# A fifth gated product moved to ScalarE and GpSimd, two small products on part of TensorE's rows, and a new order

## The chip, the core and the metric

The kernel runs on one core of a Trainium2 chip. The metric is the device time of one execution in microseconds (us). The core has five engines, each with its own in-order queue: TensorE (PE in the profile) multiplies matrices out of SBUF into PSUM; VectorE (DVE), ScalarE (ACT) and GpSimd (POOL) work elementwise; SyncE (SP) here only issues DMAs. They are ordered among each other by semaphores alone. Of PSUM's eight banks of 128x512 f32, four ("work0" to "work3") rotate among all the products, two are g_bank and two are du_bank.

## The reference

For x of 16 sequences ("batches") of 1024 positions and 256 channels:

```
def ffn(x):  h = silu(x @ wg.T) * (x @ wu.T); return h @ wd.T      # 256 -> 768 -> 256, integer weights / 127
def mamba(x):
    z, params = x @ W_z.T, x @ W_params.T                          # params: 64 for dt, 16 unused, 16 for C
    dt = softplus(params[..., :64] @ W_dt.T + b_dt)
    u  = silu(causal_conv4(x, conv_w))
    # for each of 16 states n and 256 channels e, along the 1024 positions:
    #   h[t+1] = exp(dt A) h[t] + (exp(dt A) - 1) / A * u[t]
    y  = sum_n C[n] * h[n];  return ((y + u * D) * silu(z)) @ W_out.T
x = x + 0.5 * ffn(layernorm(x)); x = x + mamba(layernorm(x)); x = x + 0.5 * ffn(layernorm(x))
```

## The kernel before, in words

Channels (of which there are two halves h of 128) lie on the partitions for the recurrence, and positions run along the free axis, in two chunks c of 512 for the matrix products. All 16 batches are unrolled, and several are in flight: while batch b's recurrence runs, the first feed-forward network of batch b+1 and the second of batch b-2 or so fill the other engines.

The recurrence of a batch is 32 units (16 states by two halves). A unit is: `ex` on ACT (decay = exp(dt A), line 1042), a DMA `bc` that spreads a row of C over the partitions (SP), `scan` on DVE (tensor_tensor_scan over 1024 positions, line 1281), `cm` on DVE (the scan's result times 1/A times C, into one of TERMS = 2 buffers, line 1317), and `cm` on POOL (adding it to acc, line 1121). The scan runs on differences of u, and the part of y that this leaves out is made by one product per half and chunk, `rm` (line 847): params' C rows (partitions 64 to 79) times a small matrix 1/A. `ai` and `aj` (DVE, lines 1253 and 1259) take it from PSUM into acc. The first and the last batch run their scans in halves of 512.

A feed-forward network has for each chunk six products `ga` and six `up` (PE, line 781; four f16 matmuls each, 128x128 by 128x512), then for each of the six parts m: `si` on ACT (silu of ga, line 924), and up times silu in one of two ways. For m in OWN, `sh` on DVE multiplies out of PSUM in one instruction (line 1234). For m in POOLED, `sc` on ACT copies up out of PSUM (line 932), and `hp` on POOL multiplies it by the silu in SBUF (line 1089). `dn` (PE, line 793) then multiplies all six parts of a chunk by wd. The up product's PSUM bank is free after `sh` or `sc`.

dt is made by `dt` on PE (line 840): a matmul of wdt_t by params over all 128 partitions. Rows 0 to 63 hold W_dt, row 96 of wdt_t holds b_dt with a row of ones in params, and the rest are zeros. `rm` likewise uses wrm_t over all 128 partitions, zero outside rows 64 to 79. `da` (ACT, lines 1000 to 1005), `dl` (ACT, lines 1012 to 1017) and `dp` (POOL, lines 1076 to 1081) make the softplus; they need another activation table than silu does, and ACT loads a table (line 860) wherever its order goes from one set to the other.

The order is written out by hand: tables (ROW for every batch; HEAD, SECOND, LATE and TAIL for batches 0, 1, 14 and 15) give each event a place, in units of a recurrence unit; `schedule()` sorts all events by it, and each engine takes the events that are its own in that one order. The four banks go to products in that order too (`Counts`, the bank that comes free first by place).

```
POOLED = {1: (0, 1, 2, 4), 2: (0, 1, 2, 4)}
OWN = {f: tuple(m for m in range(HM) if m not in POOLED[f]) for f in POOLED}
```

Of the kernel before, what the change touches and what calls it, by code (L numbers as in the profile page):

```python
# [65 lines left out]
C_ROW, ONE_ROW = 64, 96  # L66
# [72 lines left out]
    "gate": [19.958, 32.034],  # L139
    "scan": [0.213, 1.117, 2.593, 4.358, 5.349, 7.197, 7.625, 8.34, 9.445, 10.358, 11.389, 11.995, 13.207, 13.906,  # L140
        15.384, 15.903, 16.687, 18.32, 19.159, 19.899, 20.145, 20.943, 21.856, 22.753, 23.339, 24.496, 25.654, 26.37,
        27.576, 28.502, 29.719, 31.321],
    "cm": [0.763, 2.558, 3.307, 4.92, 5.936, 7.602, 7.645, 9.259, 9.973, 11.247, 11.68, 12.76, 13.675, 14.855, 15.701,
        16.238, 17.889, 19.05, 19.701, 20.074, 20.454, 21.836, 22.241, 23.055, 23.983, 24.827, 25.814, 27.11, 27.713,
        28.928, 30.427, 31.538],
    "bc": [-1.292, -0.471, 1.458, 1.927, 2.074, 2.339, 2.605, 3.54, 3.597, 5.394, 5.595, 6.81, 7.858, 7.893, 12.423,
        12.62, 13.422, 14.507, 15.09, 15.693, 17.865, 19.808, 20.366, 20.415, 20.994, 21.672, 21.766, 22.738, 24.616,
        26.245, 26.666, 29.544],
    "ex": [-0.864, 0.407, 0.698, 2.552, 2.752, 3.176, 4.127, 7.005, 7.156, 8.287, 8.437, 9.472, 12.612, 12.613,
        13.633, 13.837, 14.032, 14.734, 14.892, 15.535, 20.244, 20.502, 21.59, 21.848, 22.003, 22.603, 23.104, 23.195,  # L150
        23.408, 24.045, 26.871, 29.393],
    "op": [36.6, 36.073, 36.94, 40.339],
    "rc": [35.127, 34.564, 36.399, 40.194],
    "ra": [34.909, 35.474, 39.379, 41.765],
# [15 lines left out]
    "T2": [-15.367, 4.54],  # L170
    "Te2": [-20.05, 2.156],
    "ga1": [-82.598, -69.485, -56.827, -53.465, -52.215, -34.173, -35.219, -29.252, -28.985, -22.303, -21.242,
        -16.595],
    "si1": [-58.331, -72.212, -58.391, -50.493, -49.241, -46.574, -37.798, -27.857, -31.608, -23.71, -19.783, -19.2],
    "up1": [-84.097, -72.985, -62.385, -50.056, -47.935, -32.398, -31.353, -27.452, -24.043, -21.497, -14.128,
        -11.262],
    "sc1": [-86.862, -66.411, -70.046, -47.336, -37.827, -26.261, -25.69, -18.657],
# [12 lines left out]
    "dt": [-10.318, 10.19, -2.737, 15.485],  # L190
    "da": [-16.899, 6.405, -12.887, 11.631],
    "dl": [-14.958, 9.24, -11.602, 12.717],
    "dp": [-10.273, 9.633, -9.525, 12.01],
    "rm": [0.73, 16.404, -0.749, 18.186],
    "ai": [0.111, 12.635, -10.309, 16.146],
    "aj": [0.623, 13.391, -7.852, 18.484],
    "u0": [-11.158],
    "dt0": [-8.994],
    "d": [-8.345, 11.96],
    "db": [-6.135, 13.086],  # L200
    "gate": [14.708, 31.922],
    "scan": [-3.781, 0.11, 1.556, 2.829, 3.481, 4.451, 5.102, 5.805, 6.741, 7.694, 8.338, 8.954, 9.864, 10.183,
        12.705, 13.767, 14.812, 16.319, 18.496, 19.822, 20.516, 20.961, 22.117, 22.793, 23.175, 24.454, 24.679,
        25.637, 28.915, 29.55, 31.209, 31.699],
# [1150 lines left out]
```

## Time and profile before

| | |
|---|---|
| median of 3 runs | 2249.23 us (2248.78 to 2249.27) |
| profiled execution's own time | 2249.76 us |
| its span, first to last instruction | 2248.0 us |
| granted TensorE clock, mean | 0.979 |
| instructions | 27771 |

Busy time is the union of an engine's instruction spans. Matmuls overlap in a pipeline, so a PE that looks busy may still have short gaps in its stream; these are read from the distance between the starts of two matmuls. The whole falls into a head up to the first scan at 80.9 us, batch 0's recurrence up to 218.9 us, fourteen batches alike, the last batch from 2067.7 us, and a tail after the last scan starts at 2197.3 us.

### The profile page before, as it was taken

Reading aid. Unit: us, or ns where it says so; the run is one execution under the profiler, and the core shown is the slowest. Engines: PE = TensorE matmul, PEld = TensorE weight load, DVE = VectorE, ACT = ScalarE, POOL = GpSimd, SP = SyncE. Lnnn points to the kernel's source line nnn. Section 1 sums busy time; section 2 is a strip of 40 time slices with the busy share of each in tenths; the row PEclk is TensorE's granted clock in tenths of the full one; section 3 lists DMA queues with packets and bytes.
Section 4 is the critical chain, followed back from the end, with each engine's and each line's share of the span. In section 5 each row is a group of like instructions: output and inputs, shape, how many; then the busy total and the mean of one; then the engine's idle time right before and its main releaser. Section 6 shows DMA issues by size and latency. Waiting matters only on the chain.

```text
span 2248.0 us, 27771 instructions
## 1 busy us (share of the span) xinstructions
PE 2122.2 (94%) x8708; PEld 1282.5 (57%) x8708; DVE 2125.0 (95%) x2297; ACT 1957.5 (87%) x2900; POOL 1885.0 (84%) x1446
## 2 busy tenths in 40 slices
PE   7977999999999999999999999999999999998488
PEld 4543656656565665656566565656656565565245
DVE  2699999999999999999999999999999999999992
ACT  5989898999989899898989989899898989996782
POOL 2688889898988989898898988889899888988663
PEclk9988999999999999999999999999999999999689
DMA  2122343444344344434444443444444444433120
GB/s 93 58 66 84 133 151 132 158 143 150 123 159 145 129 160 141 151 132 150 141 142 151 141 150 133 149 142 141 151 145 140 149 142 142 146 133 121 61 75 29
DMA packets 112024, 291.15 MB, mean 130 GB/s; under 512 B 11201, under 2 KB 45314, under 8 KB 111874
## 3 DMA queue, kind: packets, MB, share of 16 engines
q1 hardware_dynamic: 111874, 289.35, 37.8%
q8 instruction: 69, 1.13, 0.2%
q14 instruction: 81, 0.66, 0.1%
HBM read 271.49 MB, written 17.83 MB: 129 GB/s over the span
## 4 chain that ended last, share of the span: by engine, by line
PE 34%; DVE 17%; ACT 15%; issue 13%; POOL 10%; DVEq 0%; POOLq 0%; ACTq 0%
PE work L793 14%; PE work L781 11%; DVE g_bank L1281 9%; POOL acc L1121 7%; DVE ring L1317 5%; ACT ring L1042 4%; ACT L860 3%; PE work L810 3%; ACT xt_lo L911 2%; PE work L803 2%; PE work L761 1%; POOL hid L1089 1%; PE work L847 1%; ACT hid L932 1%; ACT odd L924 1%
## 5 line engine op out<-in xcount | busy, mean ns | idle before, releaser
L1281 DVE TENSOR_TENSOR_SCAN g_bank<-du_bank,ring 128x1024 f32<-128x1024 f32 (+1 forms) x512 | 1099.0, 2152 | 6.4 <-ACT ring L1042 1.4
L1121 POOL TENSOR_TENSOR acc<-acc,ring 128x1024 f32<-128x1024 f32 x512 | 1023.8, 2000 | 70.1 <-DVE ring L1317 44.4
L793 PE MATMUL work<-wd_t,hid 128*128 128x256 f32 x3072 | 679.8, 379 | 3.5 <-DVE hid L1234 2.9
L1317 DVE SCALAR_TENSOR_TENSOR ring<-g_bank,inv_a,ring 128x1024 f32<-128x1024 f32 (+1 forms) x576 | 660.5, 1152 | 10.1 <-POOL acc L1121 7.6
L793 PEld LDWEIGHTS work<-wd_t,hid 128*128 128x128 f32 x3072 | 583.7, 190 | 108.2 <-issue 20.7
L1042 ACT ACTIVATE ring<-dt,a_coef 128x1024 f32<-128x1024 f32 (+1 forms) x576 | 582.7, 1047 | 8.2 <-DVE g_bank L1281 7.1
L1089 POOL TENSOR_TENSOR hid<-hid,odd 128x512 f32<-128x512 f32 x256 | 277.8, 1094 | 131.6 <-ACT hid L932 94.0
L781 PE MATMUL work<-xt_hi,wg_t 128*128 128x512 f16 x768 | 296.3, 386 | 15.6 <-ACT hid L932 6.7
L781 PE MATMUL work<-xt_hi,wu_t 128*128 128x512 f16 x768 | 294.5, 383 | 15.6 <-ACT odd L924 8.4
L860 ACT ACT_TABLE_LOAD x231 | 296.4, 1283 | 4.1
L781 PE MATMUL work<-xt_lo,wg_t 128*128 128x512 f16 x768 | 295.3, 385 | 0.0
L781 PE MATMUL work<-xt_lo,wu_t 128*128 128x512 f16 x768 | 294.2, 383 | 0.0
L924 ACT ACTIVATE odd<-work 128x512 f32<-128x512 f32 x384 | 220.3, 597 | 60.3 <-PE work L781 58.6
L832 PE MATMUL work<-xt,tap_diag 128*128 128x512 f32 x512 | 227.6, 592 | 0.0
L932 ACT ACTIVATE hid<-work 128x512 f32<-128x512 f32 x256 | 148.9, 588 | 18.8 <-PE work L781 10.4
L781 PEld LDWEIGHTS work<-xt_hi,wg_t 128*128 128x128 f16 x768 | 75.6, 98 | 152.0 <-ACT hid L932 23.9
L832 PEld LDWEIGHTS work<-xt,tap_diag 128*128 128x128 f32 x512 | 96.8, 189 | 112.6 <-issue 106.5
L781 PEld LDWEIGHTS work<-xt_hi,wu_t 128*128 128x128 f16 x768 | 75.6, 98 | 117.4 <-issue 20.1
L781 PEld LDWEIGHTS work<-xt_lo,wu_t 128*128 128x128 f16 x768 | 75.7, 99 | 111.0 <-issue 39.2
L803 PE MATMUL work<-wo_t,acc 128*128 128x256 f32 x512 | 124.4, 388 | 6.8 <-POOL acc L1112 6.0
L781 PEld LDWEIGHTS work<-xt_lo,wg_t 128*128 128x128 f16 x768 | 76.1, 99 | 83.4 <-issue 19.8
L810 PE MATMUL work<-xt,wz_t 128*128 128x512 f32 x256 | 122.1, 598 | 0.3 <-DVE hid L1234 0.2
(98 smaller groups left out, 2610.8 us busy)
## 6 DMA issues: line engine op xcount, KB each, us to landing
ring<-c_rows SPq DMA_DIRECT2D x448, 512.0 KB, 3.7
ring<-c_rows SPq DMA_DIRECT2D x64, 256.0 KB, 3.1
x_in<-L_attn_x SPq DMA_DIRECT2D x30, 512.0 KB, 3.9
out<-x_fin SPq DMA_DIRECT2D x30, 512.0 KB, 4.2
x_fin<-L_attn_x SPq DMA_DIRECT2D x2, 512.0 KB, 5.9
c_rows<-params SPq DMA_DIRECT2D x32, 32.0 KB, 3.3
out<-x_in SPq DMA_DIRECT2D x2, 512.0 KB, 3.0
ring<-L_ffn_w_gate SPq DMA_DIRECT2D x1, 768.0 KB, 5.8
```

The source lines that it names most:

```text
L781: last = pe.matmul(dst[:], w[:, k, m * P:(m + 1) * P], part_[:, k, :], start=(k == 0 and i == 0), stop=(k == EH - 1 and i == 1))
L793: last = pe.matmul(dst[:, j * E:(j + 1) * E], hid[:, K.unit[f, bt, c, m] % HIDS, t:t + P], wd_t[:, m, :], start=(m == 0), stop=(m == HM - 1))
L810: last = pe.matmul(dst[:], wz_t[:, k, h * P:(h + 1) * P], xt[:, k, KW - 1 + c * CH:KW - 1 + (c + 1) * CH], start=(k == 0), stop=(k == EH - 1))
L832: last = pe.matmul(dst[:], tap_diag[:, h, k, :], xt[:, h, k + c * CH:k + (c + 1) * CH], start=(k == 0), stop=(k == KW - 1))
L860: nc.scalar.preload_act_table_set(name)
L924: nc.scalar.activation(sil[:, K.at["silu", ev][1] % SILUS, :], bank(job)[:], ACT.Silu, scale=GATE_SCALE).then_inc(freed(job), 1)
L932: nc.scalar.activation(hid[:, K.unit[ev[1:]] % HIDS, :], bank(job)[:], ACT.Copy, scale=H_SCALE).then_inc(freed(job), 1)
L1042: nc.scalar.activation(dst, dt[bt % 2][:, h, t], ACT.Exp, scale=a_coef[:, h, s:s + 1]).then_inc(S["decay"], 1)
L1089: nc.gpsimd.tensor_tensor(v, v, sil[:, k, :], ALU.mult).then_inc(S["product"], 1)
L1121: nc.gpsimd.tensor_tensor(v, v, shaped(bt, cg[:, K.number[ev[1:]] % TERMS, :]), ALU.add).then_inc(S["summed"], 1)
L1281: scan = nc.vector.tensor_tensor_scan(g, du_h, d_h, first[0], ALU.add, ALU.mult)
L1317: nc.vector.scalar_tensor_tensor(v, g, inv_a[:, h, s:s + 1], c_row, ALU.mult, ALU.mult).then_inc(S["weighted"], 1)
```

## The change

One of six parts more, m = 3, is in POOLED in both networks: for it `sh` on DVE gives way to `sc` on ACT and `hp` on POOL. `dt` multiplies partitions 0 to 63 alone, `rm` partitions 64 to 79 alone, both out of one tile wk_t; b_dt is added as the bias operand of the two activations that read dt's bank; the fills of zeros and ones for wdt_t, wrm_t and params go, and so does the DMA of b_dt into row 96, for which two small DMAs put it on the partitions. All five tables have new numbers.

```diff
-POOLED = {1: (0, 1, 2, 4), 2: (0, 1, 2, 4)}
+POOLED = {1: (0, 1, 2, 3, 4), 2: (0, 1, 2, 3, 4)}
...
-    "sh1": [-27.982, -24.382, -20.207, -19.555],
+    "sh1": [-27.097, -21.572],
...
-        wdt_t, wrm_t = sb("wdt_t", [P, E]), sb("wrm_t", [P, E])
+        wk_t = sb("wk_t", [P, E])
...
-            sp.wait_ge(s_pads, 1)
-            sp.dma_start(wdt_t[ONE_ROW:ONE_ROW + 1, :], b_dt.rearrange("(o e) -> o e", o=1)).then_inc(w_landed, 16)
...
+                    sp.dma_start(dt_bias[:, h:h + 1], b_dt.rearrange("(h p o) -> h p o", p=P, o=1)[h]).then_inc(w_landed, 16)
...
-                    pe.matmul(dst[:], wdt_t[:, h * P:(h + 1) * P], params[:, c * CH:(c + 1) * CH],
+                    pe.matmul(dst[:], wk_t[0:R, h * P:(h + 1) * P], params[0:R, c * CH:(c + 1) * CH],
...
-                    pe.matmul(dst[:], wrm_t[:, h * P:(h + 1) * P], params[:, c * CH:(c + 1) * CH],
+                    pe.matmul(dst[:], wk_t[C_ROW:PROWS, h * P:(h + 1) * P], params[C_ROW:PROWS, c * CH:(c + 1) * CH],
...
-                    nc.scalar.activation(y, bank(job)[:], ACT.Abs).then_inc(S["sp_exp"], 1)
+                    nc.scalar.activation(y, bank(job)[:], ACT.Abs, bias=dt_bias[:, h:h + 1]).then_inc(S["sp_exp"], 1)
...
-                    nc.scalar.activation(sp_r[:, c, :], bank(job)[:], ACT.Relu).then_inc(freed(job), 1)
+                    nc.scalar.activation(sp_r[:, c, :], bank(job)[:], ACT.Relu,
+                                         bias=dt_bias[:, h:h + 1]).then_inc(freed(job), 1)
...
-            for t in (wdt_t[R:P, :], wrm_t[:], xt[:, :, 0:KW - 1], u[0][:, :, 0:1], u[1][:, :, 0:1]):
+            for t in (xt[:, :, 0:KW - 1], u[0][:, :, 0:1], u[1][:, :, 0:1]):
...
-            then(nc.vector.memset(params[R:P, :], 0.0))
-            nc.vector.memset(params[ONE_ROW:ONE_ROW + 1, :], 1.0).then_inc(s_pads, 1)
+            nc.vector.memset(ones[:], 1.0).then_inc(s_pads, 1)
```

What the new tables do to the order of an ordinary batch, by sorting both sets (between the first scans of batches 6 and 7):

| per batch | before | after |
|---|---|---|
| `cm` directly behind its `scan` on DVE (of 32) | 4 | 7 |
| `scan` directly behind the last `cm` on DVE (of 32) | 10 | 11 |
| `sh` on DVE | 8 | 4 |
| `sc` on ACT, `hp` on POOL, each | 16 | 20 |
| changes of activation table on ACT | 14 | 12 |
| `dt` and `rm` next to each other on PE | 2 | 2 |
| places where PE goes into or out of a `dt` or `rm`, or from one to the other | 14 | 14 |

In batches 0 and 15 the changes of table go from 16 and 17 to 15 and 17.

## Rows read from the trace of the kernel before

**Rows 1.** The page's busy time of each engine over the whole span.
```profile
PE 2122.2 (94%) x8708; PEld 1282.5 (57%) x8708; DVE 2125.0 (95%) x2297; ACT 1957.5 (87%) x2900; POOL 1885.0 (84%) x1446
```

**Rows 2.** Busy time in stretches: batch 0, a middle batch, the last batch, the tail.
```profile
core 0: us, PE busy (x) PEld busy (x) DVE busy (x) ACT busy (x) POOL busy (x), PEclk, DMA share, GB/s
80.90:218.90 138.00, 109.93 (x366) 57.17 (x364) 134.27 (x199) 121.40 (x194) 107.57 (x81) 0.88 0.23 72
...
1000.00:1132.20 132.20, 130.52 (x546) 79.46 (x545) 131.36 (x133) 120.35 (x177) 117.71 (x91) 1.00 0.42 144
2067.70:2197.30 129.60, 83.43 (x306) 49.33 (x306) 123.48 (x174) 91.32 (x137) 88.14 (x59) 0.78 0.22 69
2197.30:2248.00 50.70, 42.54 (x194) 28.64 (x194) 10.95 (x22) 15.37 (x27) 15.91 (x15) 0.99 0.09 32
```

**Rows 3.** Two lines: count, ns min/median/max, first and last start.
```profile
L980 ACT ACTIVATE dt<-dt x16: 206/218/218, 75.3 to 2059.5; 128x2 f32<-128x2 f32 x16
...
L847 PE MATMUL work<-params,wrm_t x128: 592/592/1222, 77.7 to 2060.2; 128*128 128x512 f32 x128
```

**Rows 4.** Groups of instructions: count, busy us, mean ns, idle time before them.
```profile
L1234 DVE SCALAR_TENSOR_TENSOR hid<-odd,work 128x512 f32<-128x512 f32 x128 | 86.6, 676 | 35.4 <-PE work L781 27.1 <-ACT odd L924 8.3
L932 ACT ACTIVATE hid<-work 128x512 f32<-128x512 f32 x256 | 148.9, 588 | 18.8 <-PE work L781 10.4 <-PE work L793 8.3
L1089 POOL TENSOR_TENSOR hid<-hid,odd 128x512 f32<-128x512 f32 x256 | 277.8, 1094 | 131.6 <-ACT hid L932 94.0 <-ACT odd L924 37.6
L860 ACT ACT_TABLE_LOAD x231 | 296.4, 1283 | 4.1
```

**Rows 5.** VectorE in order of time in a middle batch: start us, length us, instruction.
```profile
903.18 0.68 DVE L1234 SCALAR_TENSOR_TENSOR hid<-odd,work 128x512 f32<-128x512 f32 x1
903.77 2.29 DVE L1281 TENSOR_TENSOR_SCAN g_bank<-du_bank,ring 128x1024 f32<-128x1024 f32 x1
906.10 1.28 DVE L1317 SCALAR_TENSOR_TENSOR ring<-g_bank,inv_a,ring 128x1024 f32<-128x1024 f32 x1
907.42 2.30 DVE L1281 TENSOR_TENSOR_SCAN g_bank<-du_bank,ring 128x1024 f32<-128x1024 f32 x1
909.62 0.40 DVE L1192 BATCH_NORM_STATS2 stats<-x_fin 128x6 f32<-128x256 f32 x1
...
913.77 1.27 DVE L1317 SCALAR_TENSOR_TENSOR ring<-g_bank,inv_a,ring 128x1024 f32<-128x1024 f32 x1
914.95 0.42 DVE L1192 BATCH_NORM_STATS2 stats<-x_mid 128x6 f32<-128x256 f32 x1
```

**Rows 6.** TensorE in order of time in a middle batch: start, length, instruction, count.
```profile
905.13 10.52 PE L793 MATMUL work<-wd_t,hid 128*128 128x256 f32 x48
915.49 1.04 PE L761 MATMUL work<-ident,normed 128*128 128x128 f32 x8
916.37 0.38 PE L781 MATMUL work<-xt_hi,wg_t 128*128 128x512 f16 x1
...
957.08 0.38 PE L781 MATMUL work<-xt_lo,wu_t 128*128 128x512 f16 x1
957.29 1.88 PE L823 MATMUL work<-xt,wp_t 128*80 128x512 f32 x4
959.01 3.60 PE L832 MATMUL work<-xt,tap_diag 128*128 128x512 f32 x8
...
973.66 7.03 PE L832 MATMUL work<-xt,tap_diag 128*128 128x512 f32 x16
980.53 0.38 PE L781 MATMUL work<-xt_hi,wu_t 128*128 128x512 f16 x1
```

**Rows 7.** Who waited for whom in the middle batch: us, times, longest.
```profile
POOL hid L1089 <- ACT hid L932: 4.2, 3, 2.6
...
POOL acc L1121 <- DVE ring L1317: 1.3, 2, 0.7
```

More of the change, by code:

```diff
@@ L65 @@
 OUT_SCALE = 1.0 / Q
-C_ROW, ONE_ROW = 64, 96
+C_ROW = 64
 PROWS = C_ROW + N
 ROW = {
[60 rows of a table removed]
[L139 to L154, printed above, removed]
[60 rows of a table added]
+    "gate": [18.967, 32.939],
+    "scan": [1.713, 2.257, 2.986, 4.146, 4.572, 5.864, 7.012, 7.944, 9.04, 9.371, 9.903, 10.488, 11.413, 12.548,
+        13.986, 14.924, 15.326, 16.515, 17.338, 20.028, 21.592, 22.338, 23.077, 24.46, 26.143, 26.895, 28.276, 29.192,
+        29.513, 30.542, 31.1, 32.213],
+    "cm": [1.732, 2.653, 3.608, 4.305, 5.35, 6.496, 7.48, 8.646, 9.251, 9.496, 10.037, 10.555, 11.872, 13.299, 14.429,
+        14.956, 16.331, 17.075, 19.594, 20.924, 22.058, 23.075, 24.297, 25.159, 26.486, 27.703, 28.432, 29.244,
+        30.033, 30.795, 31.451, 32.477],
+    "bc": [-4.2, -4.16, -4.006, -3.21, 0.386, 0.915, 1.732, 2.182, 2.392, 3.187, 3.301, 3.753, 4.304, 5.867, 6.113,
+        6.19, 7.682, 8.527, 9.387, 10.17, 11.075, 11.154, 11.157, 15.289, 15.297, 15.546, 15.886, 17.945, 19.042,
+        19.336, 19.853, 23.54],
+    "ex": [0.178, 0.564, 1.216, 1.894, 1.916, 2.557, 4.626, 5.295, 5.57, 6.13, 6.151, 6.363, 11.173, 11.707, 12.11,
+        12.438, 12.466, 12.481, 13.956, 14.355, 20.173, 21.199, 21.509, 21.737, 22.117, 24.504, 26.081, 26.294,
+        28.025, 29.706, 30.926, 31.546],
+    "op": [35.434, 37.665, 38.094, 40.995],
+    "rc": [34.012, 34.754, 35.23, 39.134],
+    "ra": [34.239, 35.401, 38.637, 42.266],
@@ L170 @@
[L170 to L177, printed above, removed]
@@ L190 @@
[L190 to L204, printed above, removed]
@@ L211 @@
-    "ex": [-8.608, -6.948, -6.05, -5.862, -5.855, 4.815, 4.873, 6.05, 6.076, 7.394, 7.638, 7.925, 7.967, 8.908,
-        11.188, 12.662, 13.589, 13.668, 14.752, 14.895, 15.559, 17.738, 19.621, 20.167, 20.251, 20.554, 21.038,
-        24.989, 25.313, 27.508, 27.709, 30.016],
+    "sj1": [-387.901, -356.697, -344.097, -296.764, -288.913, -264.857, -254.411, -219.314],
+    "ln1": [-275.223, -195.556],
+    "lr1": [-155.576, -144.062],
+    "lx1": [-242.188, -132.422],
+    "T1": [-133.328, -72.186],
@@ new lines @@
+    "Te1": [-164.432, -72.268],
+    "Ts1": [-125.334, -62.84],
+    "Tl1": [-145.91, -62.687],
+    "sj2": [-72.591, -67.207, -48.943, -41.538, -17.684, -14.93, -11.969, -10.384],
+    "ln2": [-41.102, -10.247],
+    "lr2": [-60.509, -12.932],
+    "lx2": [-37.296, -4.509],
+    "T2": [-38.61, 0.718],
+    "Te2": [-37.221, -0.303],
+    "ga1": [-109.896, -104.426, -89.445, -78.956, -73.427, -71.163, -43.782, -42.324, -39.773, -37.955, -27.025,
+        -16.68],
+    "si1": [-110.23, -116.044, -104.464, -74.437, -67.206, -63.217, -61.921, -55.489, -53.129, -36.069, -31.275,
+        -29.214],
@@ new lines @@
+    "up1": [-100.363, -99.877, -85.23, -84.23, -74.024, -61.949, -46.579, -38.732, -38.609, -34.552, -34.243,
+        -13.399],
+    "sc1": [-81.282, -109.585, -99.71, -90.591, -72.871, -60.615, -41.92, -35.684, -32.141, -34.513],
+    "hp1": [-94.81, -136.005, -141.235, -123.565, -70.446, -57.912, -55.432, -54.024, -42.459, -39.977],
+    "sh1": [-81.724, -26.095],
+    "dn1": [-57.404, -56.835, -9.131, -7.992],
+    "rs1": [-62.779, -62.62, -18.344, -16.105],
+    "rp": [-69.661, -65.874, -29.164, -26.921],
@@ new lines @@
+    "pm": [-33.635, 2.485],
+    "pe": [-34.314, 0.93],
+    "cw": [-25.519, -9.579],
+    "cv": [-18.27, 13.668, -15.382, 14.595],
+    "us": [-29.139, 7.38, -26.157, 8.195],
+    "z": [14.392, 14.521, 13.665, 14.729],
+    "zs": [7.516, 8.299, 6.526, 9.413],
+    "dt": [-19.009, 3.89, -12.409, 18.794],
+    "da": [-29.876, 4.451, -25.087, 9.53],
+    "dl": [-29.689, 4.911, -22.362, 10.797],
+    "dp": [-38.898, 1.881, -36.432, 9.856],
+    "rm": [-10.724, 19.613, -12.307, 14.763],
+    "ai": [-22.206, 10.113, -24.612, 5.756],
@@ new lines @@
+    "aj": [-21.514, 11.09, -21.899, 9.505],
+    "u0": [-25.56],
+    "dt0": [-18.61],
+    "d": [-37.361, 5.706],
+    "db": [-18.761, 11.885],
+    "gate": [16.192, 34.043],
+    "scan": [-20.353, -12.568, -10.188, -8.53, -4.075, -3.217, -1.657, -1.25, -0.515, 0.788, 2.068, 3.005, 4.064,
+        5.342, 10.624, 11.441, 14.111, 16.388, 17.639, 19.619, 20.426, 21.029, 21.512, 21.871, 22.431, 23.811, 26.418,
+        27.533, 29.718, 29.853, 31.559, 32.56],
+    "cm": [-17.648, -11.754, -9.72, -8.118, -3.975, -2.93, -1.384, -1.081, 0.3, 1.5, 2.191, 3.075, 4.626, 7.645,
+        10.875, 12.309, 14.52, 16.456, 17.673, 19.624, 20.517, 21.283, 21.526, 22.049, 22.745, 23.921, 27.401, 27.794,
+        29.806, 30.137, 31.647, 33.701],
@@ new lines @@
+    "bc": [-22.003, -20.4, -20.249, -14.875, -13.449, -9.893, -9.856, -8.768, -7.776, -5.161, -4.537, -0.877, 0.64,
+        0.685, 3.84, 4.593, 4.767, 6.956, 9.237, 9.286, 10.145, 10.276, 10.542, 11.831, 13.456, 17.393, 18.653,
+        19.334, 20.433, 22.717, 26.552, 27.458],
+    "ex": [-18.534, -17.323, -16.727, -6.736, -0.326, 0.275, 0.459, 1.334, 2.804, 4.433, 5.215, 5.538, 5.541, 7.778,
+        7.966, 10.997, 11.267, 12.593, 12.836, 13.343, 13.717, 14.317, 14.925, 15.941, 16.229, 16.866, 18.018, 20.076,
+        21.473, 21.527, 28.816, 31.247],
@@ L249 @@
-    "zs": [-1.007, 4.337, 5.547, 11.264],
-    "dt": [-6.237, -6.058, -1.385, -4.164],
-    "da": [-11.111, -10.953, -3.604, -6.002],
-    "dl": [-5.549, -9.873, -2.707, -4.263],
-    "dp": [-5.386, -9.003, -2.63, -4.436],
-    "rm": [-2.629, -1.527, -3.197, -0.48],
-    "ai": [-5.778, -5.883, -6.449, -3.278],
-    "aj": [-2.577, -5.595, 1.0, -2.635],
-    "u0": [-6.096],
-    "dt0": [-1.571],
+    "sj1": [-101.526, -89.664, -84.422, -83.375, -70.436, -70.115, -68.598, -67.105],
+    "ln1": [-72.468, -63.986],
@@ new lines @@
+    "lr1": [-87.228, -70.016],
+    "lx1": [-67.762, -48.865],
+    "T1": [-60.689, -39.201],
+    "Te1": [-66.181, -43.768],
+    "Ts1": [-52.284, -36.733],
+    "Tl1": [-64.094, -38.931],
+    "sj2": [-29.098, -28.232, -23.773, -23.4, -18.3, -16.614, -15.401, -14.934],
+    "ln2": [-19.073, -14.814],
+    "lr2": [-20.241, -15.955],
+    "lx2": [-18.774, -16.607],
+    "T2": [-11.59, -10.019],
+    "Te2": [-17.22, -16.425],
+    "ga1": [-42.345, -41.537, -35.661, -34.644, -34.217, -33.835, -34.833, -32.361, -30.89, -28.82, -22.326, -13.985],
@@ new lines @@
+    "si1": [-51.124, -52.582, -38.526, -34.213, -36.056, -33.14, -36.978, -32.671, -28.986, -28.416, -24.252,
+        -23.136],
+    "up1": [-44.016, -41.856, -40.643, -39.411, -38.689, -31.938, -35.189, -31.266, -23.953, -22.406, -17.596,
+        -13.468],
+    "sc1": [-56.411, -52.398, -44.875, -43.887, -42.772, -37.686, -31.004, -30.244, -26.816, -24.813],
+    "hp1": [-64.735, -47.989, -44.484, -38.234, -38.452, -44.317, -32.056, -30.838, -28.943, -28.918],
+    "sh1": [-37.737, -21.608],
@@ new lines @@
+    "dn1": [-23.069, -20.97, -11.982, -11.883],
+    "rs1": [-27.933, -25.556, -20.885, -18.466],
+    "rp": [-34.767, -26.823, -22.017, -18.494],
+    "pm": [-11.409, -9.105],
+    "pe": [-16.359, -15.877],
+    "cw": [-21.533, -13.545],
+    "cv": [-7.812, -6.318, -7.531, -4.243],
+    "us": [-8.978, -11.079, -8.654, -9.172],
+    "z": [10.324, 5.906, 6.416, 13.613],
+    "zs": [8.71, 2.816, 3.639, 9.639],
+    "dt": [-9.241, -9.007, -3.116, -4.136],
+    "da": [-15.362, -13.753, -4.195, -8.098],
@@ L259 @@
+    "dl": [-14.603, -12.28, -3.84, -7.345],
+    "dp": [-9.462, -10.261, -2.915, -7.755],
+    "rm": [-1.984, -3.883, -8.106, 2.181],
+    "ai": [-1.091, -4.444, -4.502, 2.069],
+    "aj": [-0.192, -3.986, 0.684, 2.645],
+    "u0": [-7.747],
+    "dt0": [-0.37],
 }
 LATE = {
[20 rows of a table removed]
[20 rows of a table added]
 }
 TAIL = {
[19 rows of a table removed]
-    "gate": [15.254, 44.043],
-    "scan": [-0.319, 0.278, 0.623, 1.403, 2.382, 3.653, 5.734, 6.239, 7.481, 9.201, 9.722, 10.891, 11.786, 12.922,
-        14.222, 14.507, 15.214, 15.567, 16.279, 18.584, 20.236, 21.371, 22.376, 24.181, 25.341, 27.461, 29.689,
-        32.064, 34.041, 35.127, 36.83, 39.326],
@@ L314 @@
-    "ex": [0.802, 1.479, 1.687, 2.664, 3.071, 3.088, 3.396, 5.612, 5.697, 5.885, 6.371, 6.883, 7.3, 7.778, 9.361,
-        9.592, 9.67, 11.252, 15.483, 16.846, 17.11, 18.659, 20.09, 20.234, 20.425, 22.32, 22.83, 26.878, 28.561,
-        33.456, 33.752, 34.973],
-    "op": [20.494, 24.225, 53.337, 54.333],
-    "rc": [16.63, 19.283, 45.948, 48.68],
-    "ra": [15.756, 20.623, 56.439, 56.856],
[19 rows of a table added]
+    "gate": [20.075, 65.881],
+    "scan": [1.295, 2.306, 2.847, 4.031, 7.258, 8.112, 9.075, 9.872, 10.504, 10.807, 11.979, 12.281, 12.343, 13.184,
+        15.056, 17.372, 17.792, 20.534, 22.398, 23.231, 28.471, 32.713, 36.093, 39.195, 40.704, 42.028, 42.676,
+        47.145, 48.341, 54.999, 58.796, 60.92],
@@ new lines @@
+    "cm": [1.549, 2.449, 3.876, 6.405, 7.884, 8.778, 9.372, 10.022, 10.668, 11.373, 11.998, 12.296, 12.44, 14.083,
+        16.441, 17.761, 19.93, 20.891, 22.399, 27.524, 30.903, 33.057, 36.865, 40.12, 40.755, 42.463, 44.84, 48.133,
+        48.663, 58.548, 60.266, 65.147],
+    "bc": [-8.291, -4.714, -2.747, 8.503, 11.188, 11.549, 11.761, 12.111, 13.936, 14.947, 15.55, 17.751, 19.282,
+        20.406, 21.225, 22.813, 24.784, 26.389, 27.908, 33.999, 38.276, 39.089, 39.966, 60.034, 60.726, 62.727,
+        69.926, 79.698, 81.515, 84.993, 86.916, 110.724],
@@ L320 @@
+    "ex": [-0.086, 1.246, 1.909, 2.27, 2.541, 3.889, 5.22, 5.84, 7.245, 7.267, 8.781, 9.599, 11.542, 11.761, 11.956,
+        16.416, 16.754, 19.719, 21.931, 23.81, 26.937, 27.175, 31.24, 32.251, 32.88, 33.005, 40.278, 48.337, 51.826,
+        51.827, 63.136, 63.776],
+    "op": [27.484, 29.349, 78.22, 80.408],
+    "rc": [27.191, 29.695, 84.667, 89.314],
+    "ra": [25.823, 26.577, 91.894, 104.369],
 }
@@ L564, in macaron_kernel @@
         part_ident = sb("part_ident", [P, P], F16)
-        consts = sb("consts", [P, 2 * TJ + 1 + EH + 1])
+        FLAG = 2 * TJ + 1 + 2 * EH
+        consts = sb("consts", [P, FLAG + 2])
         minus_half, eps = consts[:, 0:TJ], consts[:, TJ:2 * TJ]
         ones, d_skip = consts[:, 2 * TJ:2 * TJ + 1], consts[:, 2 * TJ + 1:2 * TJ + 1 + EH]
+        dt_bias = consts[:, 2 * TJ + 1 + EH:2 * TJ + 1 + 2 * EH]
         a_coef = sb("a_coef", [P, EH, N])
@@ L572, in macaron_kernel @@
         carry = sb("carry", [P, 2, N, EH, 1])
-        flag = consts[0:1, 2 * TJ + 1 + EH:].bitcast(I32)
-        flag_f = stats[0:1, 0, 0, 0:1]
+        flag = consts[0:1, FLAG:FLAG + 1].bitcast(I32)
+        flag_f = consts[0:1, FLAG + 1:FLAG + 2]
         inv_a_u = hid[:, 0, 0:EH * PROWS].rearrange("p (h n) -> p h n", h=EH)
@@ L655, in freed @@
             return free[K.bank[job]]
-        LANDED = 16 * 9
+        LANDED = 16 * 10
         block = ctx.enter_context(nc.Block())
@@ L677, in _ @@
                 (wp_t[:, :, C_ROW:C_ROW + N], W_params[:, R + N:R + 2 * N].rearrange("(k p) m -> p k m", p=P)),
-                (wdt_t[0:R, :], W_dt),
+                (wk_t[0:R, :], W_dt),
                 (wz_t[:], W_z.rearrange("(k p) e -> p k e", p=P)),
@@ L1151, in _ @@
             nc.vector.memset(meanvar[:, :, :, 2:3], -1.0)
-            then(nc.vector.memset(params[R:P, :], 0.0))
-            nc.vector.memset(params[ONE_ROW:ONE_ROW + 1, :], 1.0).then_inc(s_pads, 1)
+            nc.vector.memset(ones[:], 1.0).then_inc(s_pads, 1)
             then(nc.vector.memset(inv_a_u, 0.0))
-            then(nc.vector.memset(ones[:], 1.0))
             dve.wait_ge(s_exp, 1)
```

70 lines of the change are left out of this document (1 added, 69 removed), and 196 rows, old and new, of tables (LATE, ROW, TAIL).

## The prediction

> **What bounds the kernel now.** I read four views in this order. First the page's busy time [rows 1]: DVE 95% and PE 94% of the span, ACT 87%, POOL 84%. Two engines look full, so averages don't tell which sets the pace. Second, an instruction that comes once a batch, the first row of [rows 3]: its sixteen starts lie (2059.5 - 75.3) / 15 = 132.3 us apart. Third, the stretches [rows 2]: in a middle batch of 132.20 us DVE is busy 131.36 us and idle 0.84. In batch 0 and in the last one DVE is the busiest too (134.27 of 138.00, 123.48 of 129.60), with PE far behind. Only the tail belongs to PE (42.54 of 50.70).
>
> Fourth, PE's stream, because its lengths overlap and flatter it. In [rows 6] 48 matmuls of 128x256 f32 start 915.49 - 905.13 = 10.36 us apart in all, 0.216 each; an f16 one of 512 columns takes 0.21; sixteen passes of 128x512 f32 take 980.53 - 973.66 = 6.87, 0.429 each; eight of 128x128 take 916.37 - 915.49 = 0.88, 0.110 each. By the loops (an f32 product is two passes) a batch has 192 for ga and up, 192 for dn, 32 for op and 8 for the low parts at 0.216 (91.6 us), 72 at 0.429 for cv, z, pm, dt and rm (30.9 us), and 48 at 0.110 (5.3 us): 127.8 us of 132.2. So PE has 4.4 us a batch in hand, DVE less than one. DVE sets the period; PE is close behind.
>
> **The change, part by part.**
>
> *The fifth pooled product, on DVE.* An `sh` takes 903.77 - 903.18 = 0.59 us of DVE from start to start [rows 5] (its 676 ns in [rows 4] overlap the next instruction). Four go per batch, 64 in all. Those that count lie between the first and the last scan: two each from the first networks of batches 1 to 15 and from the second ones of batches 0 to 14, thus 60. 60 x 0.59 = 35.4 us, 2.36 a batch.
>
> *The order, on DVE.* `cm` needs its scan's result. Right behind the scan it starts 906.10 - 903.77 = 2.33 us after it; with another instruction between, that one starts 909.62 - 907.42 = 2.20 after the scan [rows 5]. So a bare neighbour costs 0.13. A scan right behind a `cm` costs 907.42 - 906.10 = 1.32 against 914.95 - 913.77 = 1.18 with something between, 0.14. The removed `sh` were also such fillers: sorted, the new tables have three more bare pairs of the first kind and one more of the second, 3 x 0.13 + 0.14 = 0.53 us a batch, 7.4 in fourteen and, at half that in the two batches of half scans, some 8 in all. The net of DVE is 35.4 - 8 = 27.4 us, 1.83 a batch; the floor of the period falls from 132.2 to 130.4.
>
> *ACT.* Four `sc` more at 588 ns are 2.35 us; two table loads fewer at 1283 ns are 2.57 [rows 4]. ACT goes from 120.35 busy us a batch [rows 2] to 120.1 of 130.4, 92%. Nothing, and DVE is its cover. In batch 0 it is one load less, in the last none.
>
> *POOL.* Four `hp` more at 1094 ns [rows 4] are 4.38 us: from 117.71 [rows 2] to 122.1 of 130.4, 94%. Its idle time falls from 14.5 to 8.3 us a batch. Behind an `hp` that waits for its `sc` is the `cm` addition, and behind that DVE's `cm` two units later, as there are two buffers. In the middle batch POOL waited 4.2 us for ACT's copies and 1.3 for DVE [rows 7], well within 8.3. I take 0.2 us a batch, 3 in all, for this closer coupling; the bounds are nothing and the slow rival below.
>
> *dt and rm on part of the rows.* The trace has no product on fewer than 128 partitions. The nearest row is the one with fewer columns: pm (128*80) starts 957.29 - 957.08 = 0.21 us behind a full product and leaves to one after 959.01 - 957.29 = 1.72 for four passes, 0.43 each, no more than a full one [rows 6]. So I take nothing. The bounds: at best the two neighbouring dt-rm pairs of a batch run side by side, each product being 2 x 0.429, and save 2 x 0.86 = 1.7 us of PE; at worst each of the 14 places where the kind of product changes makes PE finish before it goes on. An rm pass is 592 ns long in the median [rows 3], while starts are 429 apart [rows 6], thus 0.163 us a place, 2.3 a batch. Either is PE's alone, whose 127.8 stand under 130.4.
>
> The Trainium skill speaks against this change here: "TensorEngine Tiling (Array Packing)", section Tiling Modes, says that going over to another tiling mode, not just another tile, empties TensorE first. By it the worst bound is the case, and PE needs 127.8 + 2.3 = 130.1 of the 130.4. No run here shows it yet.
>
> *Bias, fills, DMAs.* The bias rides on two activations that are there anyway. The two fills and the DMA that go, and the two small DMAs that come, are in the first 15 us, before the weights are used; ACT and PE work on batch 0's first network there. Nothing; at most 1 us either way.
>
> *Head and tail.* Before the first scan DVE isn't the bound, so the two `sh` of batch 0's first network that go bring nothing. In the tail PE is [rows 2], and the last part, m = 5, stays with DVE, so that the last product needs no trip through ACT and POOL. Nothing, give or take 2 us.
>
> *Sum*, against the profiled execution's own time of 2249.76 (span 2248.0 and 1.8 around it): 2249.8 - 35.4 + 8 + 3 = 2225.4. That execution is 0.5 above the median of its runs, so 2225.
>
> **Rivals.**
>
> *PE becomes the bound, no change.* If row-limited products cost 2.3 us a batch and PE keeps half of its present 4.4 us of gaps, which come from waiting for ACT to free banks, the period is 127.8 + 2.3 + 2.2 = 132.3: 2250, give or take 6. For it: PE is already 127.8 of 132.2, and a period nearer to its work leaves it less room for waits. Against: most gaps of a slack engine close when it becomes the bound, and pm shows no cost.
>
> *POOL becomes the bound, slower.* The place is POOL's queue in the feed-forward stretch: `hp` waits for `sc`, and the accumulating `cm` of the recurrence stands behind it, so DVE's `cm` waits for "summed". POOL's busy time would be 122.1; as long as its idle time stays under 8.3 us a batch, DVE leads; over 10.1 the kernel is slower than before. Now it is 14.5. If it only falls to 12, the period is 134.1: 14 x 1.9 = 27 us more, about 2276. For it: in the whole run POOL waits 94.0 us for `sc` results [rows 4], and every fourth more asks for more of them. Against: in the middle batch these are only 4.2 us [rows 7]; the rest is in head, tail and batch 0, where they cost nothing.
>
> *More than forecast.* The neighbours run side by side, PE needs 126.1, and the order hides its bare pairs behind waits that go: the full 2.36 us a batch and something of the 0.84 idle, 2249.8 - 35.4 - 4 = 2210, give or take 5. The Trainium skill has the mechanism in "TensorE: Matmul & The Clock Gate", Part 3: products in different row groups overlap, while a lone one of few rows is no shorter. For it: dt has rows 0 to 63, rm 64 to 79, in different banks. Against: PE's gain helps DVE only where DVE waits, which is 0.84 us.
>
> *Row limits do nothing at all*, the same instructions by time: that is within the forecast, as I cost them at nothing.
>
> **Chances.** Forecast (2217 to 2236) 0.55; more 0.13; PE the bound 0.18; POOL the bound 0.14. A measurement tells 0.2%, 4.5 us, from no change. Faster by more than that: 0.55 + 0.13 + 0.4 of PE's 0.18 = 0.75; within: 0.10, nearly all from PE's case; slower: the POOL case and a little of PE's, 0.15. The range is 2206 to 2257: it leaves out 0.03 below and about 0.13 above.
>
> **What would show it.** DVE: 4 `sh` a batch, scans 130.4 to 130.8 us a batch apart, DVE's idle time under 1.2 us in it. ACT: 203 table loads (14 batches with two fewer). POOL: 320 `hp`, 122 us a batch. PE: passes of dt and rm still 0.429 apart, and the next product right behind. The forecast fails if a middle batch's DVE idle time rises over 2.5 us: look then at whether "POOL acc" or "PE work" ended its waits (or ACT's decay, starved by ACT's own waits for PE). If dt and rm stand off their neighbours by 0.1 us or more, the emptying is real. If the batch's period is as said but the time isn't, head or tail moved.

## The result and the profile after

The changed kernel takes 2265.3 us (2263.4 to 2265.5, 4 runs) against 2249.2 before: a ratio of 1.007 with a 95% interval of 1.0053 to 1.0087. It is slower by 16 us, where 24 us less was forecast. The profiled execution's span is 2263.7 us (before 2248.0).

First the page's busy time, to be read beside [rows 1], then the groups that answer to [rows 4], with their counts.

```profile
PE 2150.3 (95%) x8708; PEld 1274.8 (56%) x8708; DVE 2089.9 (92%) x2229; ACT 1965.2 (87%) x2936; POOL 1946.9 (86%) x1510
...
L1234 DVE SCALAR_TENSOR_TENSOR hid<-odd,work 128x512 f32<-128x512 f32 x64 | 43.7, 682 | 70.5 <-PE work L782 70.0 <-issue 0.5
L861 ACT ACT_TABLE_LOAD x203 | 260.4, 1283 | 3.6
```

DVE does 35 us less, as the sum said, and POOL 62 more (64 `hp` of 1.094 us would be 70), and ACT is about where it was (8 more). But PE, which got no product more, is busy 28 us longer, and the 64 `sh` that are left wait 70.0 us for PE's up products where 128 waited 27.1.

Then the stretches, with [rows 2] beside them: batch 0, a middle batch, the last batch, the tail.

```profile
85.60:228.80 143.20, 119.47 (x377) 60.05 (x376) 133.03 (x196) 124.51 (x200) 110.57 (x84) 0.86 0.24 69
...
1028.40:1161.20 132.80, 131.73 (x546) 79.02 (x545) 129.37 (x130) 120.62 (x179) 121.57 (x95) 1.00 0.43 143
...
2088.40:2211.70 123.30, 76.22 (x291) 43.72 (x291) 121.89 (x171) 93.74 (x141) 90.15 (x61) 0.81 0.24 73
2211.70:2263.70 52.00, 44.45 (x204) 31.05 (x202) 9.82 (x20) 13.16 (x24) 18.14 (x17) 1.00 0.09 31
```

The edges are starts of first and last scans, so the span splits. Up to the first scan: 85.6 - 80.9 = +4.7. Batch 0: +5.2. Batches 1 to 14: (2088.4 - 228.8) - (2067.7 - 218.9) = +10.8. Last batch: -6.3. Tail: +1.3. Sum +15.7. In the middle batch DVE is busy 129.37 us, 2.0 less than before, but idle 3.4 instead of 0.84; one `sh` accounts for most of it (VectorE in order of time; the bracket is idle time and what ended it):

```profile
1144.71 0.69 DVE L1234 SCALAR_TENSOR_TENSOR hid<-odd,work 128x512 f32<-128x512 f32 x1 [2.69 <-PE work L782]
```

Why PE is late stands in its own order of time. The first group of rows is PE's matmuls around a `dt` (now L841, 64 rows), the second the weight loads of the same microseconds; [rows 6] has full products.

```profile
1105.40 3.70 PE L833 MATMUL work<-xt,tap_diag 128*128 128x512 f32 x8
1109.03 1.12 PE L841 MATMUL work<-params,wk_t 64*128 64x512 f32 x2
1110.08 2.42 PE L833 MATMUL work<-xt,tap_diag 128*128 128x512 f32 x5
```

```profile
1108.08 0.19 PEld L833 LDWEIGHTS work<-xt,tap_diag 128*128 128x128 f32 x1 [0.24 <-issue]
1109.03 0.29 PEld L841 LDWEIGHTS work<-params,wk_t 64*128 64x128 f32 x2 [0.76 <-issue]
1110.08 0.30 PEld L833 LDWEIGHTS work<-xt,tap_diag 128*128 128x128 f32 x2 [0.76 <-issue]
```

Two passes of `dt` take 1110.08 - 1109.03 = 1.05 us from start to start where two full ones take 0.86, and the load ends an idle time of 0.76 instead of 0.24. The third group is the same place in e2 below, where `dt` has all 128 rows (weight loads; dt is L826 there):

```profile
1087.45 0.19 PEld L818 LDWEIGHTS work<-xt,tap_diag 128*128 128x128 f32 x1 [0.24 <-issue]
1087.88 0.19 PEld L826 LDWEIGHTS work<-params,wdt_t 128*128 128x128 f32 x1 [0.24 <-issue]
1088.31 0.19 PEld L826 LDWEIGHTS work<-params,wdt_t 128*128 128x128 f32 x1 [0.24 <-issue]
1088.74 0.19 PEld L818 LDWEIGHTS work<-xt,tap_diag 128*128 128x128 f32 x1 [0.24 <-issue]
```

There `dt`'s first matmul starts at 1088.31, and its weights went in at 1087.88, while the matmul ahead streamed: a load every 0.43 us, each hidden. In the changed kernel the load of `dt`'s first pass starts only at 1109.03, with the pass itself, and so does that of the first full pass behind it, at 1110.08. The second load of each pair follows 0.11 us later, under the first pass. So two things are paid where the rows in use change: the stream stops (0.09 us), and the first pass has its weight load in the open (0.53 us to the second pass instead of 0.43).

Over thirteen middle batches the distances between starts give 0.09 us more at each of the 14 places where the kind changes, and 0.104 more behind the first pass of each row-limited product (8 a batch). 8 x 0.104 + 14 x 0.09 = 2.1 us a batch. Matched matmul by matmul with e2, the full f32 products that follow a `dt` pay for their first pass too: 0.104 behind the one at 1110.08 and behind one `dn`, 0.055 behind a transpose, 0.26 in all. f16 products pay nothing there. Together that is 2.4 us a batch.

### The profile page after: what moved, and what is told of

Same layout as the page of the kernel before. It is cut to its first block and busy times, and to the rows that moved or that the text cites. A ratio compares the mean times of both kernels' runs of the same rounds, so it can differ in the third digit from the quotient of the medians.

```text
span 2263.7 us, 27746 instructions
## 1 busy us (share of the span) xinstructions
PE 2150.3 (95%) x8708; PEld 1274.8 (56%) x8708; DVE 2089.9 (92%) x2229; ACT 1965.2 (87%) x2936; POOL 1946.9 (86%) x1510
## 5 line engine op out<-in xcount | busy, mean ns | idle before, releaser
L1091 POOL TENSOR_TENSOR hid<-hid,odd 128x512 f32<-128x512 f32 x320 | 346.4, 1093 | 86.4 <-ACT odd L925 56.0
L933 ACT ACTIVATE hid<-work 128x512 f32<-128x512 f32 x320 | 188.7, 592 | 77.2 <-PE work L782 71.5
L833 PE MATMUL work<-xt,tap_diag 128*128 128x512 f32 x512 | 232.5, 602 | 0.7 <-ACT u L970 0.7
L833 PEld LDWEIGHTS work<-xt,tap_diag 128*128 128x128 f32 x512 | 95.0, 190 | 133.3 <-issue 121.3
```

The costliest lines, as they stand in the source:

```text
L833: last = pe.matmul(dst[:], tap_diag[:, h, k, :], xt[:, h, k + c * CH:k + (c + 1) * CH], start=(k == 0), stop=(k == KW - 1))
L933: nc.scalar.activation(hid[:, K.unit[ev[1:]] % HIDS, :], bank(job)[:], ACT.Copy, scale=H_SCALE).then_inc(freed(job), 1)
L1091: nc.gpsimd.tensor_tensor(v, v, sil[:, k, :], ALU.mult).then_inc(S["product"], 1)
```

## The experiments

Times are medians; "before" ran beside each version on its chip, at 2248.9 to 2249.5. e1 to e4, e5 to e8 and e9 to e11 ran on three different chips. The bias on the activations and its DMAs stay as in the changed kernel in all of them.

| | order | pooled parts | dt and rm | us | ratio to before (95%) | us a middle batch |
|---|---|---|---|---|---|---|
| before | old | 4 | 128 rows | 2249.2 | 1 | 132.20 |
| e1 | old | 4 | 64, 16 | 2268.1 | 1.0081 (1.0064 to 1.0097) | 133.33 |
| e3 | old | 5 | 128 | 2292.0 | 1.0187 (1.0170 to 1.0204) | 134.90 |
| e4 | old | 5 | 64, 16 | 2316.2 | 1.0297 (1.0280 to 1.0314) | 137 in eight, 135.3 to 135.6 else |
| after | new | 5 | 64, 16 | 2265.3 | 1.0070 (1.0053 to 1.0087) | 132.77 |
| e2 | new | 5 | 128 | 2228.5 | 0.9906 (0.9890 to 0.9923) | 130.70 |
| e5 | new | 5 | 80, 80 | 2230.1 | 0.9912 (0.9895 to 0.9928) | 130.70 |
| e6 | new | 5 | 64, 128 | 2251.5 | 1.0007 (0.9997 to 1.0016) | 132.21 |
| e7 | new | 5 | 128, 16 | 2244.8 | 0.9982 (0.9972 to 0.9992) | 131.65 |
| e8 | new | 5 | 64, 64 | 2237.5 | 0.9944 (0.9928 to 0.9961) | 131.08 |
| e9 | new | 5 | 64, 64 in pairs alone | 2222.8 | 0.9885 (0.9867 to 0.9903) | 130.20 |

**e1, the row limits alone.** The changed kernel with before's tables and POOLED.

```diff
-POOLED = {1: (0, 1, 2, 3, 4), 2: (0, 1, 2, 3, 4)}
+POOLED = {1: (0, 1, 2, 4), 2: (0, 1, 2, 4)}
```

> The row-limited dt and rm (and the bias) alone, on the old order and four pooled parts. Both theories expect TensorE's passes of dt and rm 0.53 us apart instead of 0.43 and about 0.09 us more at each of the 14 places where TensorE enters or leaves them, 2.1 us a batch. Theory A (these weight loads, no longer hidden, are what made the change slower): TensorE's 4.4 us of gaps a batch are mostly tied to other waits, so half or more of the 2.1 us reaches the period: 2249 + 15 to 30 = 2264 to 2279. Theory B (the new order's own waits are the cause, and TensorE's spare time takes the 2.1 us up): 2248 to 2254.

2268.1, +19: theory A. 1.1 us reach the ordinary period although PE had 4.4 us of gaps; batch 0 takes 3.7 more (141.7 for 138.0).

This run also shows what the extra time belongs to. In its batch 0 two `dt` products, four passes on 64 rows, stand next to each other. PE's matmuls, then the weight loads, in order of time:

```profile
174.38 1.98 PE L825 MATMUL work<-params,wk_t 64*128 64x512 f32 x4
176.29 1.12 PE L817 MATMUL work<-xt,tap_diag 128*128 128x512 f32 x2
```

```profile
174.38 0.29 PEld L825 LDWEIGHTS work<-params,wk_t 64*128 64x128 f32 x2 [0.76 <-issue]
174.92 0.19 PEld L825 LDWEIGHTS work<-params,wk_t 64*128 64x128 f32 x1 [0.24 <-issue]
175.35 0.19 PEld L825 LDWEIGHTS work<-params,wk_t 64*128 64x128 f32 x1 [0.24 <-issue]
176.29 0.30 PEld L817 LDWEIGHTS work<-xt,tap_diag 128*128 128x128 f32 x2 [0.76 <-issue]
```

The passes start at 174.38, 174.92, 175.35 and 175.78, the full product behind them at 176.29: steps of 0.53, 0.43, 0.43 and 0.52. The third and fourth pass have their loads hidden like full ones. So 64 rows as such don't keep a load from starting early; the 0.104 belongs to the first pass behind a stop. The kernel before has it as well, on 128 rows, where `dt` had waited:

```profile
426.68 1.13 PE L840 MATMUL work<-params,wdt_t 128*128 128x512 f32 x2 [0.25 <-ACT xt L898]
427.64 0.38 PE L781 MATMUL work<-xt_hi,wu_t 128*128 128x512 f16 x1
```

427.64 - 426.68 = 0.96 = 0.53 + 0.43. Between 300 and 2000 us all 12 `dt` of the kernel before that start behind such a wait have 0.53 between their passes, the 39 others 0.43.

**e2, full rows in the changed kernel.**

```diff
-        wk_t = sb("wk_t", [P, E])
+        wdt_t, wrm_t = sb("wdt_t", [P, E]), sb("wrm_t", [P, E])
...
-                    pe.matmul(dst[:], wk_t[0:R, h * P:(h + 1) * P], params[0:R, c * CH:(c + 1) * CH],
+                    pe.matmul(dst[:], wdt_t[:, h * P:(h + 1) * P], params[:, c * CH:(c + 1) * CH],
...
-                    pe.matmul(dst[:], wk_t[C_ROW:PROWS, h * P:(h + 1) * P], params[C_ROW:PROWS, c * CH:(c + 1) * CH],
+                    pe.matmul(dst[:], wrm_t[:, h * P:(h + 1) * P], params[:, c * CH:(c + 1) * CH],
```

> The changed kernel with dt and rm over all 128 partitions again (zero-padded weights, as before); fifth pooled part, bias and new order stay. Theory A: the period falls from 132.8 by up to 2.1 us, to 130.7 to 131.5, and batch 0 shortens too: 2235 to 2247. Theory B: TensorE's passes are 0.43 apart again but VectorE's waits stay, period 132.3 to 132.8: 2258 to 2265.

2228.5: 37 us less than the changed kernel and 21 less than before, beyond what theory A had said. The ordinary period falls by 2.07 us (29 us in 14 batches), batch 0 by 4.3, the head by 1.6. The `sh` that waited 2.69 us for PE waits 0.89 here. DVE is idle 1.5 us:

```profile
1008.20:1138.90 130.70, 129.68 (x546) 79.76 (x544) 129.18 (x130) 120.36 (x179) 121.51 (x95) 1.00 0.44 146
```

**e3, the fifth part alone, on the old order.** Its `sc` and `hp` stand where the old trace has the `sh` they replace.

```diff
-    "sh1": [-27.982, -24.382, -20.207, -19.555],
+    "sh1": [-24.382, -19.555],
-    "sc1": [-34.21, -31.112, -28.501, -27.83, -25.852, -25.568, -22.962, -21.819],
+    "sc1": [-34.21, -31.112, -28.501, -28.871, -27.83, -25.852, -25.568, -22.962, -21.083, -21.819],
```

> The fifth pooled part alone: dt and rm over all rows, old order with sc and hp of part 3 put where the old trace has the time of the sh that they replace. If VectorE's 0.59 us for each sh is what counts, as the prediction has it: 2249 - 35 + 8 = 2222 to 2232. Rival C (GpSimd or the longer way through ScalarE holds the bank and the recurrence back): 2250 or more. The two table loads that the new order saves are not saved here, so ScalarE carries 2.4 us more a batch, 93 percent of the period.

2292.0, rival C: the same relief of DVE, placed in this way, makes the old order 43 us slower. DVE is idle 5.1 us of a middle batch, 0.84 before. Half of that is what my slow rival named, `cm` on DVE behind POOL, which was 0.3 us before (waits in us, times, longest):

```profile
DVE ring L1301 <- POOL acc L1107: 2.5, 2, 1.7
DVE x_fin L1226 <- PE work L778: 0.7, 1, 0.7
DVE hid L1218 <- ACT odd L909: 0.4, 1, 0.4
DVE g_bank L1265 <- ACT ring L1028: 0.4, 1, 0.4
```

**e4, both on the old order.** e3's tables in the kernel with row limits.

> Fifth pooled part and row-limited dt and rm, on the old order. Theory A: e3 plus 15 to 30 us. Theory B: e3 plus 0 to 6 us, since the row limits only use up spare time of TensorE; then the rest of the 2265 is the new order's.

2316.2, 24 more than e3, within theory A's range. So the row limits cost 19, 24 and 37 us on the three bases, and the dearest is the one with least room on PE (in a middle batch PE is idle 1.0 us in e2, 1.7 before, 4.0 in e3). About half of e4's 24 is something else: in eight ordinary batches its period is 137 and not 135.3 to 135.6, each with a fall of TensorE's clock (last section).

**e5, 80 rows for both.** The weights are zero where a product has none; the same rows of params.

```diff
-wdt_t[:, h * P:(h + 1) * P]   -wrm_t[:, h * P:(h + 1) * P]
+wdt_t[0:PROWS, ...]           +wrm_t[0:PROWS, ...]            (e5)
+wdt_t[0:R, ...]                                               (e6)
                               +wrm_t[C_ROW:PROWS, ...]        (e7)
+wdt_t[0:R, ...]               +wrm_t[C_ROW:P, ...]            (e8)
```

> e2 (new order, five pooled parts) with dt and rm both on partitions 0 to 79, the weights padded with zeros. Theory D (the weight load of a product on at most 64 partitions, a part of the array, is not begun under the matmul ahead of it, nor the next load under that product; the count of rows as such costs nothing): passes 0.43 us apart, time as e2, 2225 to 2231. Theory E (any count under 128 does it): passes 0.53 apart, 2255 to 2266.

2230.1, and the period is e2's to 0.01 us, as theory D had it and not E: 80 rows cost what 128 do. But this doesn't show D's cause, a load on at most 64 rows that is never begun early. The four passes in e1 speak against it. A price for each change between 128 (or 80), 64 and 16 rows fits all of these runs.

**e6 and e7, dt alone and rm alone.** As the diff above says, the other product on all rows.

> e2 with dt alone on 64 partitions, rm on all. Half the passes and, in this order, 8 of the 14 places where the kind changes: if cost goes by product, 1.1 us a batch, and no fall of TensorE's clock in ordinary batches, since half of the array's rows are in use where the clock fell: 2228 + 15 to 19 = 2243 to 2248. If the period has spare room for it: 2230 to 2235.

> e2 with rm alone on 16 partitions (64 to 79), dt on all. By product the same 1.1 us a batch: 2243 to 2248, and with e6 the two add up to e0's 37 less the clock's part: three falls of 3.4 us at half clock in ordinary batches cost 1.64 us each there, 4.9 in all. If the clock falls follow the 16-row product, one or more stay here and the time is up to 5 higher.

2251.5 and 2244.8: e6 lay above its range, e7 in it. For itself each product adds the same to PE's stream (4 x 0.104 + 8 x 0.09 = 1.1 us). What differs is what stands behind it: four full f32 products follow a dt of 64 rows and pay for their first pass (0.37 us together), one follows an rm (0.10), the rest are f16. Matched with e2, PE's stream is 1.5 us a batch longer in e6 and 1.2 in e7. The period is 1.51 longer for dt and 0.95 for rm; the kernels lose 23 and 16 us. That adds up to 39 for the changed kernel's 37, since the two changes between a dt and an rm are counted in both. Neither clock falls in an ordinary batch; of the three falls that e7's expectation counts, the first (at 226.6) is at the end of batch 0.

**e8, the same tile height for both.** The diff above; rm's weights are zero from row 80.

> e2 with dt on partitions 0 to 63 and rm on 64 to 127 (weights zero from 80): the same tile height, different row groups. If it is the change of tile size that costs (the Trainium skill's rule on modes), dt and rm next to each other and the second pass of each pay nothing: 10 full-to-part places of 0.09 stay, 0.9 us a batch, 2238 to 2246, and by its rule on row groups neighbours may even run side by side. If any product on part of the array pays, whatever stands beside it: as the changed kernel, 2258 to 2268.

2237.5, just under its range (of the 14 places 12 stay, not 10). The neighbours did more than pay nothing; they ran together. TensorE in order of time, rm L833 and dt L826:

```profile
1101.66 0.38 PE L767 MATMUL work<-xt_lo,wg_t 128*128 128x512 f16 x1
1101.97 0.69 PE L833 MATMUL work<-params,wrm_t 64*128 64x512 f32 x1
1101.98 0.69 PE L826 MATMUL work<-params,wdt_t 64*128 64x512 f32 x1
1102.51 0.59 PE L833 MATMUL work<-params,wrm_t 64*128 64x512 f32 x1
1102.51 0.59 PE L826 MATMUL work<-params,wdt_t 64*128 64x512 f32 x1
1103.03 5.45 PE L779 MATMUL work<-wd_t,hid 128*128 128x256 f32 x24
```

Four passes in 1103.03 - 1101.97 = 1.06 us; on full rows they take 1.72. In the batch's other pair, with dt ahead, rm starts 0.16 us behind it and the four take 1.22. The first pass of a pair and of a lone `dt` keeps its 0.104. In the changed kernel rm has 16 rows and dt 64, and they follow one another:

```profile
1119.74 1.12 PE L848 MATMUL work<-params,wk_t 16*128 16x512 f32 x2
1120.79 1.12 PE L841 MATMUL work<-params,wk_t 64*128 64x512 f32 x2
1121.84 5.45 PE L794 MATMUL work<-wd_t,hid 128*128 128x256 f32 x24
```

**e9, 64 rows for neighbours alone.** e2, with this (and likewise for rm, `slice(C_ROW, P)`):

```diff
+            beside = {e for a, b in zip(mine, mine[1:]) if {a[0], b[0]} == {"dt", "rm"} for e in (a, b)}
...
+                    r = slice(0, R) if ev in beside else slice(0, P)
-                    pe.matmul(dst[:], wdt_t[:, h * P:(h + 1) * P], params[:, c * CH:(c + 1) * CH],
+                    pe.matmul(dst[:], wdt_t[r, h * P:(h + 1) * P], params[r, c * CH:(c + 1) * CH],
```

`mine` is PE's events in order.

> e2 with 64-row tiles (dt on 0 to 63, rm on 64 to 127) only where a dt and an rm stand next to each other on TensorE, two pairs a batch; the other four products on all rows. A pair side by side took 1.06 us with 0.09 of exposed load ahead of it, against 4 x 0.43 = 1.72: 0.56 us a pair, 1.1 a batch of TensorE's time. If TensorE still sets part of the period (130.70, with VectorE busy 129.28 of it), up to 1 us a batch: 2213 to 2226. If VectorE alone does: as e2, 2226 to 2230. If I am wrong on the pairs: 2230 to 2240.

2222.8, 26 us under the before beside it, and within the range for a TensorE that still sets part of the period. It is 5.7 under e2, which ran at another time on another chip: their ranges (2221.8 to 2224.4 and 2227.8 to 2229.5) don't meet, but the intervals of their ratios overlap. The surer sign is the period, 130.20 for 130.70 us, each steady to 0.02 over twelve batches. It is the fastest version. DVE is idle for 0.95 us of a middle batch, near the 0.84 before, so DVE probably sets the pace again:

```profile
1003.80:1134.00 130.20, 129.11 (x546) 78.83 (x544) 129.25 (x130) 120.31 (x179) 121.44 (x95) 1.00 0.44 146
```

**e10 and e11, which load the old order couldn't carry.** Part 3's `hp` (e10) or `sc` (e11) does 32 of 512 columns.

```diff
-                    nc.gpsimd.tensor_tensor(v, v, sil[:, k, :], ALU.mult).then_inc(S["product"], 1)
+                    w = 32 if m == 3 else CH
+                    nc.gpsimd.tensor_tensor(v[:, 0:w], v[:, 0:w], sil[:, k, 0:w], ALU.mult).then_inc(S["product"], 1)
...
-                    nc.scalar.activation(hid[:, K.unit[ev[1:]] % HIDS, :], bank(job)[:], ACT.Copy,
+                    nc.scalar.activation(hid[:, K.unit[ev[1:]] % HIDS, 0:w], bank(job)[:, 0:w], ACT.Copy,
```

> e3 (old order, fifth part pooled) with GpSimd's product of part 3 on 32 of 512 columns, so GpSimd has nearly the load of before; ScalarE keeps its copy. The other columns are left without their silu factor. If GpSimd's 4.4 us more a batch are what turned the old order to 134.9 us a batch: 130.4 to 132, total 2225 to 2250. If ScalarE's 2.4 us are: it stays at 134 to 135, 2280 to 2292.

> e3 with ScalarE's copy of part 3 on 32 of 512 columns, GpSimd's product whole (it multiplies what stood in the slot), and one fill of hid on GpSimd at the start. If ScalarE's load is the cause: 131 to 132.5 us a batch, 2235 to 2255; if GpSimd's: 134 to 135, 2280 to 2295.

2281.0 (1.0140, 1.0122 to 1.0158) and 2270.1 (1.0097, 1.0079 to 1.0115), 134.05 and 133.3 us a batch. e10 leaves 480 columns of part 3 without their silu, e11 leaves them as they stood in the slot. e10's time lies in its second range, e11's in neither. My either-or fails: taking POOL's load away gives back 11 of e3's 43 us, ACT's 22, and neither reaches before, though DVE has its relief in both. In e10 POOL is busy 118.3 of 134.0 us and `cm` still waits 1.7 us for it. So the load of one engine alone isn't the cause. Both loads together were not taken away, and no other placement on the old order was tried. That it is the place of the added instructions in two in-order queues, and what stands behind them, is argued from this and not shown.

## Why the prediction was wrong, step by step

- *What bounds the kernel:* right in that DVE set the period with PE close behind. "PE has 4.4 us a batch in hand" was wrong as a reserve: on the old order, with all of these gaps, the row limits still lengthened the period by 1.1 us (e1).
- *DVE's relief and the bare neighbours:* right. e2, the change without row limits, has a period of 130.70 for a predicted 130.4 to 130.8, with 203 table loads and 320 `hp`. A bare neighbour costs 0.12 to 0.13 us in e2 as well, and there are three and one more of them. Its 2228.5 lies 3.5 us from the 2225, and that is in part luck: against before, the head is 3.1 longer, batch 0 1.0 and the tail 1.2, and the last batch is 6.0 shorter, none of it in the sum.
- *ACT and POOL:* their loads came out as said (120.6 and 121.6 us a batch). That this costs 3 us was right for the new order only. On the old one, in e3's placement, the fifth part cost 43, about half of DVE's new idle time by the place I had named. The forecast gave the order no term but the neighbours.
- ***dt and rm on part of the rows* is the step that failed.** "So I take nothing", said the prediction, by pm's 80 columns, "no more than a full one". The row was near in kind but not in the quantity that counts: it had fewer columns, not fewer rows. The cost is 2.4 us of PE a batch, close to the bound of 2.3 that stood beside it. The sentence after it failed as well: 127.8 + 2.3 under 130.4 was taken as room, and the period rose by 2.07 us (e2 to after), 37 us in all. Part of the price could have been read before: [rows 6] has products in a full stream alone, while a `dt` behind a wait has 0.53 between its passes.
- *The emptying of the array* named by the Trainium skill ("TensorEngine Tiling (Array Packing)", Tiling Modes) gave the right side. Its modes have 128, 64 or 32 rows, and the trace agrees with it: 0.09 us at each change between 128, 64 and 16 rows, none between products on 64 (e1's four passes, e8's pairs), and nothing for 80 rows, which 64 can't hold (e5). That the bound's size came out is luck: it was 14 x 0.163 = 2.3, from the length of an rm pass, and what is paid is 14 x 0.09 and, apart from that, 1.1 us for first passes whose load lies in the open, a term that stood nowhere.
- *The rivals:* "PE becomes the bound" had 0.18 and was the one that came true by its mechanism, at 2265 rather than 2250, give or take 6: its price was half a guess on gaps, and it had no term for the clock (below), batch 0 or the head. My range ended at 2257.
- *Head and tail:* the head grew by 4.7, 3.1 of it with full rows too (84.0 in e2). The fifth part alone makes it 1.9 longer on the old order (e3), so not all of that is the new order's. The last batch got 6 us shorter in e2 and after alike, and 0.8 longer in e3: that is the new order's. I had foreseen neither.
